# Weight turns moved into a pause, register loads cut into pieces, and the experts' bias added apart from the products, in an adaLN block on one core

## The reference, cut to what matters

```python
h = layernorm(x) * (1 + ca) + sa
x = x + ga * attention(h, wq, bq, wkv, bkv, wo)        # 2 x 1024 tokens, E = 256, 16 heads of 128, 4 key heads, causal
h = layernorm(x) * (1 + cb) + sb
# mixture of 8 experts, top 2
logits = h @ gate_w.T
top_vals, top_idx = top_k(logits, 2)
w = softmax(top_vals)
y_all = einsum('td,eod->teo', h, expert_w) + expert_b
y = sum over the two chosen experts of w * y_all
x = x + gb * y
```

## Time and profile before

| | |
|---|---|
| runs | 881.04, 881.52, 883.5 us, median 881.52 |
| profiled execution | 881.51 us, of which the span of instructions is 879.8 |
| PE busy | 864.9 us (98%) |
| DVE busy | 738.7 us (84%) |
| ACT busy | 545.9 us (62%) |
| POOL busy | 326.1 us (37%) |
| chain of waits that ended last | PE 91%, DVE 4%, ACT, issue, DMA and POOL 1% each |

### The profile page before, as it was taken

One profiled execution on the slowest core, in us unless ns is written; L12 is line 12 of the kernel. 1 busy time (PEld: TensorE's weight loads), 2 busy tenths in 40 slices (PEclk: granted clock), 3 DMA queues, 4 the chain that ended last, 5 costly groups with the idle time before them and its releaser, 6 DMA issues.

```text
span 879.8 us, 17031 instructions
## 1 busy us (share of the span) xinstructions
PE 864.9 (98%) x5431; PEld 772.7 (88%) x5431; DVE 738.7 (84%) x1680; ACT 545.9 (62%) x1256; POOL 326.1 (37%) x398
## 2 busy tenths in 40 slices
PE   8999999999999999999999999999999999999997
PEld 8888898888888888888888989999888888889996
DVE  6878888888888888878878889888888989879676
ACT  5686666666666666664566666666666666675452
POOL 2744122222222222131534444444422222586575
PEclk9999999999999999999999999999999999999999
DMA  7000800000000000320000000000000000442485
GB/s 270 2 12 14 281 19 13 13 12 12 12 12 12 12 12 13 102 13 7 0 26 13 14 13 13 13 13 13 13 13 12 2 13 13 151 145 84 145 251 169
DMA packets 41362, 43.37 MB, mean 49 GB/s; under 512 B 7264, under 2 KB 38526, under 8 KB 41214
## 3 DMA queue, kind: packets, MB, share of 16 engines
q1 hardware_dynamic: 38936, 36.22, 13.4%
q0 software_dynamic: 2304, 6.29, 2.2%
q10 hardware_dynamic: 56, 0.02, 0.0%
HBM read 32.29 MB, written 15.21 MB: 54 GB/s over the span
## 4 chain that ended last, share of the span: by engine, by line
PE 91%; DVE 4%; ACT 1%; issue 1%; DMA 1%; POOL 1%; SPq 0%; POOLq 0%; ACTq 0%
PE ps_t L1117 13%; PE ps_s L1001 8%; PE ps_s L1005 8%; PE ps_s L1002 8%; PE ps_o L993 7%; PE ps_o L997 7%; PE ps_o L994 7%; PE ps_m L1001 4%; PE ps_m L1005 4%; PE ps_m L1002 4%; PE ps_m L993 3%; PE ps_m L997 3%; PE ps_m L994 3%; PE ps_o L1127 1%; PE ps_t L1001 1%
## 5 line engine op out<-in xcount | busy, mean ns | idle before, releaser
L1473 ACT ACTIVATE pt_hi<-ps_t 128x512 fp32r<-128x512 f32 (+2 forms) x320 | 170.8, 534 | 121.3 <-PE ps_t L1117 119.7
L1523 ACT ACTIVATE probs<-ps_s,neg_max 128x128 f32<-128x128 f32 (+7 forms) x256 | 189.9, 742 | 80.3 <-DVE neg_max L1930 77.8
L1939 DVE TENSOR_TENSOR pt_lo<-ps_t,pt_hi 128x512 fp32r<-128x512 f32 (+2 forms) x320 | 192.6, 602 | 13.8 <-ACT pt_hi L1473 10.1
L1930 DVE TENSOR_REDUCE neg_max<-ps_s 128x1 f32<-128x128 f32 (+7 forms) x256 | 192.6, 752 | 3.7
L738 POOL TENSOR_TENSOR q_lo<-raw,q_hi 128x512 fp32r<-128x512 f32 x60 | 77.4, 1290 | 309.1 <-ACT q_hi L1473 309.1
L1117 PE MATMUL ps_t<-ident,probs 128*128 128x128 f32 x1152 | 188.7, 273 | 0.9 <-DVE pt_lo L1939 0.9
L1117 PEld LDWEIGHTS ps_t<-ident,probs 128*128 128x128 f32 x1152 | 141.9, 141 | 20.6 <-DVE pt_lo L1939 4.9
L1001 PE MATMUL ps_s<-k_hi,q_hi 128*128 128x512 f32 (+2 forms) x354 | 148.7, 420 | 2.4 <-ACT probs L1523 2.4
L1977 DVE SCALAR_TENSOR_TENSOR acc<-ps_m,rsum,acc 128x256 f32<-128x256 f32 x256 | 111.5, 477 | 15.9 <-PE ps_m L1005 15.3
L1924 DVE TENSOR_TENSOR ps_s<-ps_s,mask 128x128 f32<-128x128 f32 x256 | 75.7, 296 | 56.9 <-PE ps_s L1005 49.3
L1005 PE MATMUL ps_s<-k_hi,q_lo 128*128 128x512 f32 (+2 forms) x354 | 123.4, 349 | 0.0
(11 more groups left out here) (344 smaller groups left out, 1721.8 us busy)
## 6 DMA issues: line engine op xcount, KB each, us to landing
slot_out_dram<-y_slot SPq DMA_DIRECT2D x38, 128.0 KB, 2.0
wq_raw<-in_L_attn_wq_dram SPq DMA_DIRECT2D x32, 128.0 KB, 2.3
wo_raw<-in_L_attn_wo_dram SPq DMA_DIRECT2D x32, 128.0 KB, 2.0
wkv_raw<-in_L_attn_wkv_dram SPq DMA_DIRECT2D x2, 1024.0 KB, 6.7
acc<-in_L_attn_x_dram SPq DMA_DIRECT2D x2, 1024.0 KB, 16.8
we_raw<-in_L_ffn_expert_w_dram SPq DMA_DIRECT2D x1, 2048.0 KB, 8.3
slot_rows<-slot_rows_dram SPq DMA_DIRECT2D x2, 1024.0 KB, 8.1
slot_rows_dram<-in_L_attn_x_dram SPq DMA_DIRECT2D x1, 1920.0 KB, 16.2
```

Of the source, the lines that this page charges most:

```text
L1473: return nc.scalar.activation(dst, src, ACT.Copy, scale=scale)
L1523: nc.scalar.activation(probs[par][:, prob_offset(i):prob_offset(i) + w], ps_s[:, i % 2, col:col + w], ACT.Exp, bias=neg_max[:, par, i:i + ...
L1930: nc.vector.tensor_reduce(neg_max[:, par, i:i + 1], ps_s[:, i % 2, col:col + w], AXIS_X, ALU.max, negate=True).then_inc(max_set, 1)
L1939: nc.vector.tensor_tensor(pt_lo[:, q % PT, lo:CH], ps_t[:, q % 2, lo:CH], pt_hi[:, q % PT, lo:CH].bitcast(F32), ALU.subtract).then_inc(pt_ ...
```

## The change

**Turns.** turn_weights writes the banks 0 and 1 of kv_bank. Turns 0 and 1 (eight transposes) stand at q = 1 of frame 31, turns 2 to 7 at q = 3 to 8. ACT scales the last two pieces at q = 3 and 4 of that frame.

**Loads.** The 23 registers are loaded in eight pieces of three (the last of two) in frame 30, one at the end of each step q = 1 to 8. The load of 15 is not touched.

**Bias.** The extra matmul of each slot and pair is gone. The two softmax weights of a token are laid out by expert (pick times weight, the two added), cut in a high, a low and again the high part, 3 x 4 tiles x 8 experts = 96 columns: stack0 for the eight first tiles (POOL in frame 31, from picks that DVE makes at its q = 0), stack1 for near tiles (POOL, behind late_row) and late tiles (DVE, behind coefficients). turn_coefs turns them (PE, two transposes each, at slot 5 and after dense (0,1)), read_coefs copies them (ACT), and eight bias_product (two matmuls of 256 columns each, over 96 rows of bias_table) give the bias of two tiles each: after slots 6 to 9 and after dense (0,2), (0,3), (1,0), (1,1). DVE adds each to acc (add_bias, 128x512), the last one ahead of slot_lower(24). slot_product(23) waits for all eight additions. The order of pairs is BIAS_PAIRS.

```diff
+PLANES = 3
+COLS = HALF * EXPERTS
+BIAS_PAIRS = [0, 1, 2, 3, 6, 7, 4, 5]
...
+SCALED_AGAIN = 3
...
+LOAD = 3
+LOADS_AT = range(1, 9)
...
+            def stack_coefs(chosen, weight, n, planes, done):
+
+                scaled = [picks[:, f, 0:n, :] for f in range(FREE)]
+                for f in range(FREE):
+                    pool.tensor_tensor(scaled[f], chosen[:, f, :, :], weight[:, f, :].unsqueeze(2).to_broadcast([P, n, EXPERTS]),
+                                       ALU.mult).then_inc(bias_step, 1)
...
+                pool.tensor_tensor(scaled[0], scaled[0], scaled[1], ALU.add).then_inc(bias_step, 1)
...
+                for v in (0, 2):
+                    pool.tensor_scalar(planes[:, :, v, :], sums, 1.0, 1.0, ALU.mult, ALU.mult).then_inc(bias_step, 1)
...
+                pool.tensor_tensor(planes[:, :, 1, :], sums, planes[:, :, 0, :].bitcast(F32),
+                                   ALU.subtract).then_inc(pool_made, 1)
...
                 if u == 0:
-                    pe.wait_ge(exp_set, NT * B * HEADS)
+                    pe.wait_ge(exp_set, NT * B * HEADS - 1)
...
-                        last = pe.transpose(kv_bank(2 + u % 2)[:, col:col + P],
+                        last = pe.transpose(kv_bank(u % 2)[:, col:col + P],
...
-                    if very_last and q == 1:
-                        pe.wait_ge(place_set, 1)
-                        first_e.extend(chosen(slot_expert_u, SLOTS))
-                    if very_last and FIRST_TURN <= q < FIRST_TURN + EXPERTS // 2 * KE:
-                        turn_weights(q - FIRST_TURN)
+                    if b + 1 == B and l + 2 == HEADS and q in LOADS_AT:
+                        if q == LOADS_AT[0]:
+                            pe.wait_ge(place_set, 1)
+                        done = LOAD * LOADS_AT.index(q)
+                        first_e.extend(chosen(slot_expert_u, min(done + LOAD, SLOTS), done))
+                    if very_last and q + 1 == FIRST_TURN:
+                        turn_weights(0)
+                        turn_weights(1)
+                    if very_last and FIRST_TURN < q < FIRST_TURN + EXPERTS // 2 * KE - 1:
+                        turn_weights(q - FIRST_TURN + 1)
...
                 if s == SLOTS:
                     pe.wait_ge(late["logits_set"], 1)
+                    pe.wait_ge(y_add, 4 * B * HEADS + len(BIAS_PAIRS))
...
-                nc.tensor.matmul(bank, bias_ones[:, :], bias_planes[:, bass.ds(e, 1), :].rearrange("p x o -> p (x o)"),
-                                 start=True, stop=False)
...
+            def turn_coefs(planes, bank):
+
+                for g in range(2):
+                    last = pe.transpose(bank[0:PLANES * COLS, g * P:(g + 1) * P],
+                                        planes[:, g, :, :].rearrange("p v c -> p (v c)").bitcast(F32), ident[:, :])
+                last.then_inc(small_mm, 1)
+
+            def bias_product(o):
+
+                first = 2 * BIAS_PAIRS[o]
+                pe.wait_ge(small_read, 1 if first < NT else 3)
+                pe.wait_ge(y_add, 4 * B * HEADS + (o if o <= NT // 2 else o - 1))
+                for i in range(2):
+                    g, k = divmod((first + i) % NT, HALF)
+                    last = nc.tensor.matmul(bias_bank(o)[:, i * O:(i + 1) * O], coef_t[:, g * P:(g + 1) * P],
+                                            bias_table[:, first // NT, k, :], start=True, stop=True)
+                last.then_inc(bias_mm, 1)
...
+                if s == 5:
+                    pe.wait_ge(pool_made, 2)
+                    pe.wait_ge(y_add, 4 * B * HEADS)
+                    turn_coefs(stack0, ps_m)
+                if 6 <= s < 10:
+                    bias_product(s - 6)
...
+                if s == 6:
+                    read_coefs(1, ps_m)
...
+                for v in (0, 2):
+                    nc.vector.tensor_copy(stack1[:, 1, v, :], sums).then_inc(coef_step, 1)
+                dve.wait_ge(coef_step, 3)
+                nc.vector.tensor_tensor(stack1[:, 1, 1, :], sums, stack1[:, 1, 0, :].bitcast(F32),
+                                        ALU.subtract).then_inc(coef_set, 1)
+
+            def add_bias(o):
+
+                dve.wait_ge(bias_mm, o + 1)
+                pair = acc[:, 2 * BIAS_PAIRS[o]:2 * BIAS_PAIRS[o] + 2, :].rearrange("p n e -> p (n e)")
+                nc.vector.tensor_tensor(pair, bias_bank(o)[:, :], pair, ALU.add).then_inc(y_add, 1)
...
+                if 7 <= s < 11:
+                    add_bias(s - 7)
                 if s + 2 < SLOTS:
                     slot_lower(s + 2)
...
             mix(1, {}, range(2, 2 * DENSE_EARLY - 2))
+            add_bias(NT // 2 + 2)
             slot_lower(SLOTS)
             mix(1, {}, range(2 * DENSE_EARLY - 2, 2 * DENSE_EARLY))
+            add_bias(NT // 2 + 3)
             slot_lower(SLOTS + 1)
```

More of the change, by code:

```diff
@@ L398, in adaln_block @@
         y_odd = moe("y_odd", [P, 2, O])
+        stack1 = moe("stack1", [P, 2, PLANES, COLS], F32R)
+        coef_t = moe("coef_t", [PLANES * COLS, 2 * P], F32R)
         y_sum = at("y_sum", [P, HALF, O], F32, pt_at)
@@ L428, in slot_bank, with bias_bank @@
             return kv_bank(s % 2) if s < SLOTS else (ps_o, ps_m)[s % 2]
+        def bias_bank(o):
+            return ps_m if o < NT // 2 or o % 2 == 0 else ps_o
         def turn_bank(u):
@@ L891, in frame @@
                 if b == 1 and l + 1 == HEADS:
+                    pool.wait_ge(t_mm, NS * (B * HEADS - 1))
+                    pool.wait_ge(r_dve, FIRST_PICKS + FREE)
+                    stack_coefs(picks, r_weight, NT, stack0, KE)
                     bias_tables()
@@ L955, in pool_join @@
                 pool.wait_ge(rows_step, done + 2)
-                pool.tensor_tensor(picked[:, 0, j, :], picked[:, 0, j, :], acc[:, j, :], ALU.add).then_inc(pool_joined, 1)
+                pool.tensor_tensor(picked[:, 0, j, :], picked[:, 0, j, :], acc[:, j, :], ALU.add).then_inc(pool_made, 1)
             inverse_deviation2(0)
@@ L970, in _ @@
                 late_row(d + 1)
+            pool.wait_ge(near["step"], 2 * HALF + 6 + HALF)
+            stack_coefs(near["pick"], near["weight"], HALF, stack1[:, 0:1, :, :], KE + 8)
             for m in range(HALF):
@@ L1428, in experts @@
                 pair = slice(2 * e2, 2 * e2 + 2)
-                nc.tensor.matmul(bank, bias_ones[:, :], bias_planes[:, pair, :].rearrange("p x o -> p (x o)"),
-                                 start=True, stop=False)
                 for k in range(KE):
                     w = [t[:, k, pair, :].rearrange("p x o -> p (x o)") for t in (we_hi, we_lo)]
-                    last = held_late(bank, (h2_hi[d % 2][:, k, :], h2_lo[d % 2][:, k, :]), w, False, k == KE - 1,
+                    last = held_late(bank, (h2_hi[d % 2][:, k, :], h2_lo[d % 2][:, k, :]), w, k == 0, k == KE - 1,
                                      (h2_lo_set, d + 1) if e2 == 0 and k == 0 else None)
@@ L1462, in _ @@
                     experts(d, e2)
+                    if d == 0 and e2 == 1:
+                        pe.wait_ge(pool_made, 3)
+                        pe.wait_ge(coef_set, 2)
+                        turn_coefs(stack1, ps_o)
+                    if 2 <= d * 4 + e2 < 6:
+                        bias_product(NT // 2 + d * 4 + e2 - 2)
                     if d == 0 and e2 == 1:
@@ L1679, in read_rank, with read_coefs @@
             def read_rank():
-                act.wait_ge(rank_mm, 1)
+                act.wait_ge(small_mm, 2)
                 nc.scalar.activation(n_rank[:, :, :].rearrange("p n e -> p (n e)"), kv_bank(3)[:, 0:(HALF + 1) * EXPERTS],
-                                     ACT.Copy).then_inc(rank_set, 1)
+                                     ACT.Copy).then_inc(small_read, 1)
+            def read_coefs(count, bank):
+                act.wait_ge(small_mm, count)
+                if count > 1:
+                    act.wait_ge(bias_mm, NT // 2)
+                keep_hi(coef_t[:, :], bank[0:PLANES * COLS, 0:2 * P]).then_inc(small_read, 1)
             def mix_first(d):
@@ L1769, in _ @@
             mix_first(0)
+            read_coefs(3, ps_o)
             hidden2_hi(2)
@@ L2050, in frame @@
                         weights_lo(q - FIRST_TURN)
+                    if b + 1 == B and l + 1 == HEADS and q == 0:
+                        dve.wait_ge(t_mm, NS * (B * HEADS - 1))
+                        for f in range(FREE):
+                            nc.vector.tensor_tensor(picks[:, f, :, :], tiles_of(iota8[:, :]),
+                                                    r_first[:, :, f:f + 1].to_broadcast([P, NT, EXPERTS]),
+                                                    ALU.is_equal).then_inc(r_dve, 1)
                     if b + 1 == B and l + 1 == HEADS and q in (9, 10):
@@ L2467, in _ @@
                     coefficients()
-            mix(0, {})
+            mix(0, {}, range(2, 6))
+            add_bias(NT // 2)
+            mix(0, {}, range(6, EXPERTS))
+            add_bias(NT // 2 + 1)
             finish(0)
```

103 lines of the change are left out of this document (61 added, 42 removed).

## The result

| | before | changed |
|---|---|---|
| median of 16 runs, us | 881.46 (880.64 to 883.5) | 883.33 (882.61 to 884.71) |
| profiled span, us | 879.8 | 881.3 |
| PE busy, us | 864.9 | 861.0 |
| DVE busy, us | 738.7 | 743.2 |

The ratio is 1.0019, 95% interval 1.0012 to 1.0025: slower by 1.9 us, clear of noise, though inside the 0.3% that the prediction called no change. The forecast was 882.3 us. In the profiles PE is busy 3.9 us less and the kernel takes 1.5 us more.

A forecast was written before the change was run, and what follows sets the result against it. PE was taken as the bound, with 98% of the span and 91% of the chain. The terms summed as 881.51 + 1.8 − 0.8 + 0.3 + 0.2 − 0.7 = 882.3 us, range 879.0 to 884.8.

The forecast's parts named there:

- Register loads, +1.8: Frame 30: eight loads of about 1.44 us lose 1.0 at the first, 0.45, 0.2 and 0.1 at three others.
- a line through both gives 0.056 us a register and 1.27 fixed: Load price from the profiled loads of 23 (2568 ns) and 15 (2118 ns), giving 1.44 us for three registers.
- Rival A: Frame 30: matmuls queued ahead cover all eight register loads, so they cost nothing; 880.5 us, chance 0.28.
- The pause, −0.8: Frame 31: earlier o_lo and transposes in PE's 1.60 us pause give 1.5, new waits at turns 2 and 4 lose 0.7.
- Slots 3 to 22, +0.3: First slot stage: twenty matmuls go (−2.4), but transposes, bias products and new waits, 0.74 at slot 6, outweigh them.
- POOL beside DVE, +0.2: Near half of stack1: six small POOL operations slow DVE's near places by sharing; +0.2 us, bounds 0 and 3.6.
- Rival D: Near half of stack1: each of six POOL operations makes DVE wait 0.25, 1.5 for 0.2; 883.6 us, chance 0.07.
- Second half, −0.7: Dense pairs and second slot stage: matmuls removed (−1.6, −1.56) outweigh transposes, products and a +1.35 wait at slot 23.
- Thirteen of slots 23 to 35: −1.56: Second slot stage: thirteen removed matmuls save 1.56 us, as the stage runs at PE's pace, 1.075 a slot.
- The end, 0: From slot 35's finish: nine removed dense matmuls leave PE but not the ACT and POOL chain, so 0 us.
- Rival B: As Rival A, and the new waits at slot 6 (0.74) and slot 23 (1.35) don't show; 878.4 us, chance 0.15.
- Rival C: Frame 30: PE's queue doesn't refill between loads, seven loads lose 0.4 more each; 885.1 us, chance 0.10.

The follow-up runs named there:

- one-load run: Changed kernel with one load of 23 registers at q = 1 of frame 30 in place of eight of three: 884.16 us, ratio 1.0035 to the kernel before.
- the first two runs: Kernel before with the eight loads only (881.49 us, ratio 1.0006), then with loads, turns and scaling as changed but the bias as before (880.71 us, ratio 0.9997).
- the loads alone: Kernel before with one edit, eight loads of three in frame 30 for the load of 23 in frame 31: 881.49 us, ratio 1.0006.
- the early additions: Changed kernel with DVE's last two bias additions each before two mixes in place of behind them: 881.57 us, changed kernel on the same chip 882.93.
- the bias alone: Changed kernel with the load, turns and scaling of the kernel before: 883.29 us, ratio 1.0027 to the kernel before.
- four reorderings of one line or two: Changed kernel with load of 15 ahead of stack1's turn, additions early, first four bias products a slot later, ACT's copies first: 879.69 us, ratio 0.9985 to kernel before.

## Why the prediction was right, and where it wasn't

The range held the time, and the side (no change by 0.3%, a little slower) was right. (The chances were given for 878.9 to 884.2, 0.3% each way, and not for the range; the time lies in both.) The sum wasn't right step by step, and that its total came within about 1 us is luck: the loads were 1.5 too dear and the second half 1.8 too cheap.

**Register loads, +1.8: measured +0.3.** The failed step is "a line through both gives 0.056 us a register and 1.27 fixed". Two rows with different surroundings don't give a line: the load of 15 took 1.69 to 2.47 us over these kernels with nothing changed in it. The first load of three takes 0.95, the others about 0.77. The proportional bound (0.34) was as wrong. The place and the start of the exposed load (q = 1, behind q_lo's wait, 759.65 forecast and 759.7 measured) were right, and it was the only one; the 0.75 forecast for three others was nothing. Rival A, not the forecast, described it, except for this one load. One load of 23 in the same place costs 1.7 (one-load run).

**The pause, −0.8: measured −0.5 (−0.6 between the first two runs).** Right in mechanism: scaling out of o_hi's way, transposes in the pause, new waits of 0.44 and 0.71 at turns 2 and 4. That the load's leaving gives nothing was shown by the loads alone.

**Slots 3 to 22, +0.3, and POOL beside DVE, +0.2: measured +0.67 together, up to the first dense matmul.** The part from x_rows on is +0.85 (27.83 to 28.68), and what lies ahead of it −0.18, which the prediction had as waited out. By starts the wait at slot 6 cost 0.74, as forecast, the rank's 0.25 (0.3 forecast) and h's 0.31 (0.48 forecast). The four pairs of bias products were under-sized, 1.28 for 0.96, and a term is missing: the five slots that start behind ACT's copy, some 0.6. POOL beside DVE is at most 0.06 of it, where 0.2 was forecast.

**The port.** Rival D would have had DVE stand behind POOL's six operations for 1.5 us. Operations with two inputs on DVE ran as in the kernel before (n_order 0.23 at 823.34, and 0.23 at 822.37 before) while POOL ran from 822.99 to 824.54, but for n_rank, 0.05 longer. The Trainium skill's page "SBUF — State Buffer", section "Who interferes with whom", has such operations contend for a port pair that is an exclusive lock; the prediction took that as the second of the two blocked for the whole of the other. At 128x32 elements the trace shows no block of that length; the pair of the earlier trace rows, 0.6 us longer on DVE beside 0.75 us of POOL, is the only place that bears it out. No run here separated the two.

**Second half, −0.7: measured +1.1.** Three things:
- The wait of slot 23 was forecast as 1.35 and cost 1.35 by starts. Right, and the early additions, which take it away, show that DVE's order caused it.
- "The load of 15 is not touched" is what the change's description says, and the prediction took it as a cost of nothing. It missed that turn_coefs and its wait for coef_set come ahead of the load in PE's queue. The load begins 3 us later, when it has 1.1 us of cover in place of 3.4: a hole of 0.63 in the changed kernel (0.89 by starts), 0.94 in the bias alone. Moving it ahead of the wait removes it.
- "Thirteen of slots 23 to 35: −1.56; there the stage runs at PE's pace." It did, at 1.08 us a slot, but the next bound lay 0.06 below: ACT copies a slot's bank out behind the next high part, and PE needs that bank for the slot two on. The stage went to 1.02 a slot, giving 0.7 of 1.56. With the copy first it went to 0.93.

**The end, 0: measured −0.2.** As forecast. (The matmul of slot 35, 0.12 of the stage's 1.56, falls in this stretch.) POOL's tables, the free edit, were done at 791.62, 7.7 us ahead of slot 0.

Rival B had both new waits hidden; they cost 0.74 and 1.35. Rival C (PE's queue doesn't refill) has no trace: seven of eight loads cost nothing. Of the prediction's own signs, the value product 0.6 sooner, the waits at slots 6 and 23 and the length of the first slot stage (32.9 forecast, 33.08 measured) came true; the loads of 1.4 us and the hole of 1 us at q = 1 didn't.

What remains open: the first stage's share of the slots that start behind ACT's copy, and the rank's and h's waits, are read from the traces and none was tried by itself; why a pair of bias products takes 0.31 to 0.34 in the first stage and 0.24 in the second isn't known.

## What to carry to other kernels

When an instruction is put with a wait ahead of something that needs time but no data from it (a register load, a DMA issue), the thing behind starts late by that wait: list what stands behind every new wait in the queue, also what the change doesn't touch. A stage at its engine's pace gives back only the distance to the next bound, so work out that bound (here the round trip of a bank through ACT) before multiplying the saving by the number of steps. Where the removed work is paid, the order on the other engines must be changed with it: four reorderings of one line or two turned +1.9 us into −1.4.

## What the runs showed of the hardware that I had not expected

The time of a register load isn't set by its count alone: 23 registers took 2.57, 2.57 and 2.32 us, 15 took from 1.69 to 2.47, three from 0.76 to 0.98, two 0.53. The first load of the eight was the long one in every kernel (0.95 to 0.98, the six others of three 0.76 to 0.78), also when the eight stood one step later (0.96). The load of 15 was shorter where PE ran out of work during it (1.69 to 2.00) than where matmuls ran beside it (2.12 to 2.47), in all kernels here. The step from two registers to three, 0.24 us, would make 23 of them over 5 us; so small and large loads don't lie on one line here.
